# Pre-norm attention and FFN on eight cores: side work ordered by a play of two clocks, VectorE's program from six streams, statistics one tile ahead

## The reference

```
x = x + attn(layernorm(x));  x = x + ffn(layernorm(x))

attn(r):  q = einsum('bnd,hkd->bnhk', r, Wq)   # 16 heads, 64 each
          k = einsum('bmd,dk->bmk', r, Wk)     # one key head
          v = einsum('bmd,dv->bmv', r, Wv)     # one value head
          a = softmax(einsum('bnhk,bmk->bnhm', q, k) / 8)
          out = einsum('bnhv,dhv->bnd', einsum('bnhm,bmv->bnhv', a, v), Wp)

ffn(r):   s = r @ Win + bin                    # 1024 -> 64
          h = relu(s[..., None] * W1 + b1)     # 64 x 16
          out = (einsum('btmh,mh->btm', h, W2) + b2) @ Wout + bout
```

## Time and profile before

| | |
|---|---|
| median of 3 runs | 975.62 us (974.95 to 975.79) |
| the profiled execution, its own time | 975.78 us |
| its span, slowest core (core 7) | 974.2 us |
| spans of the 8 cores | 972.4 to 974.2 us |
| ScalarE busy | 913.7 us (94%), 1000 instructions |
| TensorE busy | 896.4 us (92%), 11484 matmuls |
| VectorE busy | 649.2 us (67%), 938 instructions |
| GpSimd busy | 77.0 us (8%) |
| first exponential starts | 26.08 us |
| last exponential ends | 944.43 us |
| longest waits of ScalarE | for scores 15.5 us in `spa`, 9 times; for transposes in the tail 10.4; for the key weights' load 8.5; in the tail for `ob` 6.8 |
| the chain that ended last | ScalarE 81%, issue 11%, TensorE 4% |

### The profile page before, as it was taken

The page is one execution under the profiler, slowest core; times in us unless marked ns, Lnnn a source line. Parts: engine busy times, 40 slices in busy tenths (PEclk is TensorE's granted clock), DMA queues, the critical chain, the costliest instruction groups (busy, mean ns, idle before and its releaser), DMA issues.

```text
span 974.2 us, 29152 instructions; the slowest of 8 cores (972.4 to 974.2 us)
## 1 busy us (share of the span) xinstructions
PE 896.4 (92%) x11484; PEld 479.6 (49%) x11484; DVE 649.2 (67%) x938; ACT 913.7 (94%) x1000; POOL 77.0 (8%) x150
## 2 busy tenths in 40 slices
PE   4799899999999999999999999999999998998884
...
GB/s 208 139 14 88 89 107 119 125 132 2 21 26 8 26 9 13 19 7 7 51 130 14 18 18 13 18 8 28 30 136 18 18 24 7 134 64 18 50 2 43
DMA packets 46291, 48.71 MB, mean 50 GB/s; under 512 B 35152, under 2 KB 35280, under 8 KB 46160
## 3 DMA queue, kind: packets, MB, share of 16 engines
...
...
## 4 chain that ended last, share of the span: by engine, by line
ACT 81%; issue 11%; PE 4%; DVE 2%; DMA 1%; POOL 0%; DVEq 0%; SPq 0%; POOLq 0%; ACTq 0%
ACT ptu L1082 81%; PE ob L646 1%; DMA xbuf<-x_own 1%; DVE lnst L668 0%; PE spa L911 0%; DVE lnst L672 0%; PE sdb L579 0%; PE spb L948 0%; PE spb L911 0%; POOL rstd L1105 0%; DVE qt L745 0%; DVE r1u L691 0%; ACT hz L1092 0%; PE sda L568 0%; DVE gacc L1052 0%
## 5 line engine op out<-in xcount | busy, mean ns | idle before, releaser
L1082 ACT ACTIVATE ptu<-spa 128x1024 bf16<-128x1024 f32 x491 | 560.3, 1141 | 15.9 <-PE spa L911 15.5
L1082 ACT ACTIVATE ptu<-spb 128x1024 bf16<-128x1024 f32 x490 | 560.6, 1144 | 0.6 <-PE spb L911 0.5
L646 PE MATMUL ob<-vab,ptu 128*128 128x65 bf16 x7848 | 390.5, 195 | 1.0 <-DVE vab L742 0.6
L646 PEld LDWEIGHTS ob<-vab,ptu 128*128 128x128 bf16 x7848 | 285.4, 97 | 199.5 <-issue 199.5
L911 PE MATMUL spa<-qt,k2t 64*128 64x512 bf16 x982 | 192.9, 381 | 26.4 <-ACT ptu L1082 17.8
L911 PE MATMUL spb<-qt,k2t 64*128 64x512 bf16 x980 | 192.2, 380 | 20.7 <-ACT ptu L1082 19.4
L911 PEld LDWEIGHTS spa<-qt,k2t 64*128 64x128 bf16 x982 | 57.9, 92 | 116.1 <-issue 103.3
L911 PEld LDWEIGHTS spb<-qt,k2t 64*128 64x128 bf16 x980 | 59.0, 92 | 112.8 <-issue 99.4
L978 DVE TENSOR_TENSOR oacc<-oacc,ob 128x520 f32<-128x520 f32 x52 | 36.2, 696 | 71.7 <-PE ob L646 71.3
L1103 POOL TENSOR_SCALAR lnve<-lnmv 128x1 f32<-128x1 f32 x48 | 17.9, 374 | 561.1 <-DVE lnmv L674 561.1
L841 DVE SCALAR_TENSOR_TENSOR r1t<-oacc 128x1024 bf16<-128x1024 f32 x43 | 52.6, 1224 | 5.6 <-DVE oacc L836 5.2
...
## 6 DMA issues: line engine op xcount, KB each, us to landing
...
ot<-on SPq DMA_TRANSPOSE x38, 2.3
```

The lines of the kernel that those rows point to most:

```text
L646: r = te.matmul(osum[:, hd, c * 65:(c + 1) * 65], ptu[:, g % NPT, hd * 512 + c * 128:hd * 512 + (c + 1) * 128], vab[:, CHUNKS[s][i], :], s ...
L1082: sc.activation(ptu[:, g % NPT, :], sps[g % 2][:], AF.Exp, scale=0.125 / SCORE_SCALE).then_inc(ex, 1)
```

## The change

1. `pace` is written anew: instead of a lag over a budget it keeps a clock of TensorE and one of VectorE, notes for every semaphore value the time at which it will be there (with latencies `SEEN_PE`, `SEEN`, `RSTD`, and times for loads, `LOADS`, `LOADED`), moves TensorE's clock at scores to the time of the exponential that frees the buffer, and places a side piece where it ends before the next scores are due. VectorE's clock takes, of the streams that can start, the one that comes first in the list (`play_dve`).
2. VectorE's program after the first tiles is the order of that play, from six streams: `oo` (the former `o_out`), `ev`, `l0` (statistics and normalisation of key tiles, no longer tied to `evac_side`), `ln`, `ff`, `po`.
3. At the start: statistics of tile i + 1 are made ahead of the normalisation of tile i; ScalarE doubles the key weights after it has copied the first transposed tile, not before; GpSimd issues query chunk 3's weights right behind chunk 2's.
4. `phase_a_order`: query chunks 1 and 2 ahead of the transposes of slab 1, chunk 3 between them, chunk 4 behind them.

No instruction of the computation is added or taken away. Its core:

```diff
-    o = [("V", 0, 0)] + q(0, 1) + tr[:1] + q(0, 2) + tr[1:2] + q(0, 3) + tr[2:3] + q(0, 4) + tr[3:]
-    o += [("V", 1, 0)] + q(0, 5, 6, 7)
+    o = [("V", 0, 0)] + q(0, 1, 2) + tr[:2] + q(0, 3) + tr[2:] + q(0, 4) + [("V", 1, 0)] + q(0, 5, 6, 7)
...
-SWITCH = 20
+SWITCH = 10
...
+SEEN_PE = 25
+SEEN = 35
+RSTD = 125
+MOVED = {"trd": 560, "otd": 420}
+LOADED = 700
...
+AT_FIRST = {"pe": 2100, "dve": 2200}
...
+    def run_dve(w):
+        clock["dve"] = max(clock["dve"], ready_at(head[w][0])) + head[w][1]
+        order.append(w)
         head[w] = next(sides[w], None)
...
+    def play_dve(until):
...
+            can = []
+            for w in dve_sides:
+                need = need_of(w)
+                t = None if need is None else ready_at(need)
+                if t is not None:
+                    can.append((max(t, clock["dve"]), w))
+            if not can:
+                return
+            t = min(can)[0] if len(can) == 1 else min(c[0] for c in can)
+            if t > until:
+                return
+            can = [w for s, w in can if s <= t]
+            if "ff" in can and "po" in can and due and len(order) % 2:
+                can.remove("ff")
+            run_dve(can[0])
...
+            force(want, "s")
+            clock["pe"] = max(clock["pe"] + SWITCH * (mode[0] != "halves"), exp_at[g] + EXPED)
+            exp_at[g + 2] = max(exp_at[g + 1] + SLOT, clock["pe"] + SCORED)
+            clock["pe"] += SCORES
+            mode[0] = "halves"
...
+            start = max(clock["pe"], t)
+            end = start + PIECE + SWITCH * (mode[0] != ("whole" if whole else "halves")) + SWITCH * whole
+            if g + 3 < NG and not open_end:
+                limit = max(limit, ready_at(wanted(g + 3)) - 2)
+            if end > limit and not (open_end and start <= clock["pe"]):
+                break
...
+        def key_norm_side(v, note):
+
+            for li in range(4, NTILES):
+                yield [("x", li)], 62
+                ln_stats_a(v, li)
+                yield [], 96
+                ln_stats_b(v, li)
+                note("agg", li + 1)
+                yield [("agg", li + 1), ("smd", USE_NO["tr", li - 4, 0] + 1 if li >= 8 else 0)], 76
+                ln_norm(v, li)
+                note("nrm", li + 1)
...
             ln_stats(v, 0)
             ln_stats(v, 1)
             ln_norm(v, 0)
+            ln_stats(v, 2)
             ln_norm(v, 1)
-            ln_stats(v, 2)
+            ln_stats(v, 3)
             ln_norm(v, 2)
-            ln_stats(v, 3)
             ln_norm(v, 3)
...
-            sc.wait_ge(wkl, 16)
-            sc.activation(wkb[:, :, 64:128], wkb[:, :, 0:64], AF.Copy).then_inc(wkd, 1)
...
+                if step == 0:
+                    sc.wait_ge(wkl, 16)
+                    sc.activation(wkb[:, :, 64:128], wkb[:, :, 0:64], AF.Copy).then_inc(wkd, 1)
...
-                for c in {2: [1], 3: [2], 4: [3], 5: [4], 6: [5], 7: [6], 8: [7]}.get(i, []):
+                for c in {2: [1], 3: [2, 3], 4: [4], 5: [5], 6: [6], 7: [7]}.get(i, []):
```

366 lines of the change are left out of this document (197 added, 169 removed).

## The result

| | before | after |
|---|---|---|
| median of the runs | 975.79 us (5 runs) | 971.45 us (5 runs) |
| ratio | | 0.9949 (95% interval 0.9932 to 0.9966) |
| span of the profiled execution, slowest core | 974.2 (core 7) | 969.9 (core 4) |
| spans of the 8 cores | 972.4 to 974.2 | 965.8 to 969.9 |
| VectorE, ScalarE, TensorE busy | 649.2, 913.7, 896.4 | 646.1, 913.9, 900.7 |

Two of the five runs of the changed kernel (986.79 and 996.63 us) fell in the chip's slower state, and the ratio is that of the other three (970.07, 970.33 and 971.45) to the kernel before. By it the changed kernel is faster by 0.5%, some 5.0 us (3.3 to 6.6).

The account below looks back on a forecast made before the run. ScalarE's exponentials were taken as the bound, full from 105.11 to 944.43 us, so gains come earlier: 1.6 + 5.3 + 1.5 - 0.5 - 0.1 = 7.8 us off 975.62 gives 967.8 us; range 965.3 to 971.8.

Parts of the forecast that it names:

- First scores: Before the first exponential: next tile's statistics fill VectorE's idle, first scores at 24.0 instead of 25.59 us; gain 1.6 us.
- E(0) to E(20): Exponentials 0 to 20, TensorE short behind VectorE: the new order brings exponential 20 to 52.6 us; another 5.3 us gained.
- chunk 2's load is the doubtful one: Query weights ahead of exponential 4: chunk 2's load, issued earlier at 16.7, taken to land at 28.1 instead of 29.8 us.
- Rival (a): Early scores: chunk 2's weights land at 29.8 as before, chunk 1's 1.7 late; 3 us less gain, 970.8; chance 0.13.
- The value projection's wait ahead of E(20): Exponentials 16 to 20: slab 1's value projection stands whole there, its evacuation is waited for; gives back 1.6 us.
- E(20) to E(68): Exponentials 20 to 68: ScalarE's gaps ahead of exponentials 64 and 68 both go; gain 1.5 us.
- E(68) to the end: From exponential 68: no slot found heavier; late value sums at 84 segment ends cost 0.5 us, bounds 0 and 2.
- Tail: After the last exponential: half an output projection is evacuated ahead of the last reciprocal; cost 0.1 us.
- (b): Up to exponential 20: scores 8, 12, 16 and 20 each wait 1 us more behind VectorE; 4 less, 971.8; chance 0.13.
- (d): Segment ends: late value sums show 0.2 us of ScalarE at each of 84, 16.8 us, giving 984; chance 0.05.
- (e): Whole kernel: planner's clocks drift from the chip's, some 8 us lost, time within 0.2% of now; chance 0.09.
- The signs: ScalarE: score waits from 15 to 6-8 us, no gaps at exponentials 64 and 68, 1 us idle after, 29.8 us tail.

Follow-up runs that it names:

- pro_only: Kernel before with only the new start (statistics one tile ahead, key weights doubled after the first transposed tile's copy): 974.84 us, ratio 0.9997.
- wq_early: Changed kernel with query chunk 1's weight load issued behind 1/sigma of tile 1 instead of tile 2: 969.39 us, ratio 0.9935.
- late_x: Changed kernel with SyncE's loads of x tiles 8 to 11 issued after normalisation 5, not after 1 to 4: 970.75 us, ratio 0.9943.
- best: Changed kernel with chunk 1's weights issued earlier, x tiles 8 to 11 later, and 37 unused matmuls near the four gaps: 967.86 us, ratio 0.9921.
- fill2: Changed kernel plus 84 unused 512-column matmuls in slots without side work that stand behind two such slots: 969.29 us, ratio 0.9932.
- fill_680: Changed kernel plus 17 unused 512-column matmuls in slots without side work between 610 and 716 alone: 969.08 us (1 run).

## Why the prediction was right, and where it was wrong

**First scores (1.6).** Right in kind. E(0) comes 1.3 earlier in the mean, and 3.0 on the slowest cores, 26.08 to 23.06. The walk took the durations of core 7, where each group of 8 matmuls took its 0.80 to 0.85 until 23.9. On the other cores a group takes half of that from 18 to 21 us on, and on core 4 of the changed kernel from 18.65 on:

```profile
17.09 1.06 PE L986 MATMUL sda<-identb,r1u 128*128 128x128 bf16 x8
...
18.65 0.61 PE L1008 MATMUL ob<-r1t,wkb 128*128 128x128 bf16 x8
19.10 0.61 PE L986 MATMUL sdb<-identb,r1u 128*128 128x128 bf16 x8
```

The gain of the edit itself is 1.0 (pro_only), so 1.6 was too much; most of the rest of the 3.0 is that the slowest core of before was the one with the slow groups. That is luck. A term that is walked on one core carries that core's luck.

**E(0) to E(20) (5.3).** The walk was good, and one load and what followed it were not in it. It gives 28.1 us for the stretch (24.5 to 52.6), 5.3 less than the 33.41 of core 7, on which it was walked. With chunk 1's weights in time (wq_early) the stretch is 28.50: 4.9 gained on that core's time. (Against before's mean of 34.14 it is 5.6, but that mean holds the 0.8 to 1.4 us that six cores lost to the clock, which the walk did not have.) With the weights late the changed kernel has 29.81, and on its slowest core 31.29, 2.1 gained.

The step that failed is the assumption that chunk 2's load is the doubtful one and chunk 1's in time. Chunk 2's landing was well judged, 28.1 taken and 26.3 to 28.1 measured. Chunk 1's got no landing time at all. It was issued at 15.8 on core 4, behind the value weights, took 9.1 us (6.1 to 7.0 on the cores that do not wait for it) and landed at 24.9, for a consumer that the order had moved to directly behind S(0). S(0) had been walked at 24.0 and came at 22.6, so the wait eats a part of what was gained there. Of the 3.2 us that are missing on the slowest core (5.3 less 2.1), 0.4 is the walk's own, 0.8 to 1.0 the late load and the rest, 1.8 to 2.0, the granted clock behind the wait (late_x). Rival (a), with a chance of 0.13, named chunk 1 "with them" and put 3 us on the two loads by their waits alone; that this is near 3.2 is luck, since the larger part was the clock.

The value projection's wait ahead of E(20) is there: E(16) to E(20) takes 5.14 instead of 3.94 before, 1.2 given back. The prediction says 1.6 at that point, but its own times (47.3 and 52.6) give back 1.35; its sum goes by the times. E(20) itself came at 52.81 in the mean, near the 52.6 of the walk, by two misses that cancel: E(0) 1.5 earlier than walked, the stretch behind it 1.7 longer.

**E(20) to E(68) (1.5).** Right, 1.8 on every core, with no idle of ScalarE ahead of E(64) or E(68): in the window 54.35 to 98.17 above ScalarE is busy all of its 43.82 us.

**E(68) to the end (cost 0.5, bounds 0 and 2).** The term that was priced has about the right size: cores without any clock gap take 838.3 (best) against 837.7, which is 0.6. It is not spread over the 84 segment ends, though: on core 0 of best some 0.4 has come by E(190), which is not traced further, and 0.2 comes at E(619) alone, where TensorE waits 0.45 us for VectorE's evacuation at a segment's end (core 4 of the changed kernel). The step that failed is the sentence that compared the slots and looked only for heavier ones. What the new planner made is lighter ones, and the granted clock falls behind them (fill2 and fill_680 show it); that costs 0.8 to 2.5 us by core, 1.5 in the mean (839.81 less 838.3). Nothing in the bounds or among the rivals had it, and it is the reason why the time came near the end of the range.

**Tail (0.1).** Right, 29.92 against 29.77. VectorE evacuates the last projection ahead of the reciprocal, as walked:

```profile
940.18 0.69 DVE L826 TENSOR_TENSOR xbuf<-xbuf,sdb 128x512 f32<-128x512 f32 x1 [3.80 <-PE sdb L695]
940.79 0.20 DVE L954 RECIPROCAL zrec<-ob 128x8 f32<-128x8 f32 x1
```

**The rivals.** (a) came, as said. (b) did not come in its size: the waits ahead of E(12) and E(16) are 1.89 and 3.70 us, where before had 4.13 and 4.80, and wq_early, which has no wait for a load of queries, takes 0.4 more than was walked, not 4. Nor did (d), 0.6 us and not 16.8; its 0.12 us per end for the whole gain should be 0.10 (8.3 us by 84). (e) is out: the planner's order holds.

**The signs.** No idle at E(64) and E(68) and 29.9 us after the last exponential came as said. ScalarE's wait for scores did not fall to 6 to 8 us: it is still 14.6 on the slowest core, and the four waits ahead of E(4), E(12), E(16) and E(20) alone are 9.7 in wq_early. ScalarE was to be busy all but 1 us of what follows E(68), and is idle 2.0. Both signs that were named for being wrong came: TensorE waits for a weight load, and ScalarE is idle a few exponentials behind segment ends, though by the clock and not by late value sums.

**The sum.** On the slowest cores it is 7.8, less 3.2 (0.4 of the walk, the rest the load and the clock behind it), less 2.0 for the clock after E(68), plus 1.4 since the slowest core of before was slow in its prologue, and 0.3 from E(20) on: 4.3. Without that 1.4, which nothing in the forecast gave, this execution would have come out at about 972.9, past the end of the range. That the time lies in the range owes that much to luck.
